# Sparse experts: two of three block tables made between the first eight blocks; a diagonal router and a scan in the prologue

## The reference, cut to what matters

```python
flat = x.reshape(-1, C)                       # 8192 x 64
logits = flat @ router_w.T                    # 8 experts
probs = jax.nn.softmax(logits, axis=-1)
topk_probs, topk_idx = jax.lax.top_k(probs, 2)
topk_probs = topk_probs / (jnp.sum(topk_probs, axis=-1, keepdims=True) + 1e-09)
gates = jnp.einsum('nk,nke->ne', topk_probs, jax.nn.one_hot(topk_idx, 8))
h = jax.nn.silu(jnp.einsum('nc,ehc->neh', flat, w1)) * jnp.einsum('nc,ehc->neh', flat, w3)   # 682 hidden
y = jnp.einsum('neh,ech->nec', h, w2)
out = jnp.einsum('ne,nec->nc', gates, y)
```

## Time and profile before

| what | value |
|---|---|
| median of 3 runs | 2289.25 us (2287.74 to 2291.01) |
| the profiled execution | 2279.4 us, of which the trace spans 2277.6 us |
| first stage (ffn2): first SyncE load / first row load of the second block | 1186.6 / 1271.2 us |
| second stage (ffn3): the same | 1790.2 / 1873.7 us |
| mean granted TensorE clock | 0.839 of full speed |

### The profile page before, as it was taken

The page is one execution under the profiler, slowest core; times in us unless marked ns, Lnnn a source line. Parts: engine busy times, 40 slices in busy tenths (PEclk is TensorE's granted clock), DMA queues, the critical chain, the costliest instruction groups (busy, mean ns, idle before and its releaser), DMA issues. The chain is left out here.

```text
span 2277.6 us, 30440 instructions
## 1 busy us (share of the span) xinstructions
PE 1677.3 (74%) x11157; PEld 967.5 (42%) x11157; DVE 1245.0 (55%) x2416; ACT 965.8 (42%) x1715; POOL 590.1 (26%) x591
## 2 busy tenths in 40 slices
PE   2899996897999970312304599999845539999994
PEld 2433333345333340100103366666545426666663
DVE  6643335655633357578787555555462565555554
ACT  2565653333655543325123244444322424444441
POOL 0100000001000000000005577743452157776332
PEclk8899997996999975556555799999967759999997
DMA  1322210002222200000000354444268014544444
GB/s 41 76 68 65 65 56 20 0 0 50 76 65 65 65 23 0 0 0 0 0 4 27 117 147 147 149 138 134 92 152 167 7 57 149 147 146 143 133 133 151
DMA packets 117333, 175.30 MB, mean 77 GB/s; under 512 B 38106, under 2 KB 66522, under 8 KB 116674
## 3 DMA queue, kind: packets, MB, share of 16 engines
q1 hardware_dynamic: 99906, 155.38, 23.8%
q0 software_dynamic: 17280, 17.99, 2.4%
HBM read 148.60 MB, written 24.70 MB: 76 GB/s over the span
## 5 line engine op out<-in xcount | busy, mean ns | idle before, releaser
L1350 DVE TENSOR_TENSOR ffn_hidden<-ffn_silu,ffn_up_ps 114x512 f32<-114x512 f32 x426 | 293.0, 688 | 349.9 <-ACT ffn_silu L1320 349.0
L1262 PE MATMUL ffn_up_ps<-ffn_turned,ffn_weights 64*114 64x256 f32 x3408 | 445.8, 394 | 5.8 <-DMA ffn_weights<-in_ffn_weights 4.9
L1320 ACT ACTIVATE ffn_silu<-ffn_up_ps 114x512 f32<-114x512 f32 x426 | 254.4, 597 | 388.9 <-PE ffn_up_ps L1262 386.5
L826 POOL DMA_INDIRECT slots<-ffn_rows,ffn_slot x256 | 251.7, 983 | 557.4 <-DVE ffn_slot L944 386.4
L736 ACT ACTIVATE ffn_hidden<-ffn_up_ps,ffn_b 128x512 f32<-128x512 f32 x512 | 310.1, 689 | 198.0 <-PE ffn_up_ps L631 198.0
L1241 POOL DMA_INDIRECT results<-ffn_yout,ffn_xin x284 | 271.9, 957 | 246.0 <-DVE ffn_yout L1338 179.6
L1262 PEld LDWEIGHTS ffn_up_ps<-ffn_turned,ffn_weights 64*114 64x114 f32 x3408 | 288.1, 176 | 110.6 <-issue 59.6
L631 PE MATMUL ffn_up_ps<-ffn_T,ffn_up_w 64*128 64x512 f32 x1024 | 261.2, 623 | 3.1 <-ACT ffn_hidden L736 3.1
L652 PE MATMUL ffn_y_ps<-ffn_hidden,ffn_down 128*64 128x512 f32 x1024 | 247.9, 605 | 3.4 <-DVE ffn_y_total L526 3.4
L1273 PE MATMUL ffn_y_ps<-ffn_hidden,ffn_weights 114*64 114x256 f32 x1704 | 215.2, 388 | 0.0
L526 DVE SCALAR_TENSOR_TENSOR ffn_gated<-ffn_y_ps,ffn_b,ffn_gates 128x512 f32<-128x512 f32 x96 | 72.0, 751 | 204.7 <-PE ffn_y_ps L652 203.1
(11 more groups left out here) (412 smaller groups left out, 2067.1 us busy)
## 6 DMA issues: line engine op xcount, KB each, us to landing
ffn_weights<-in_ffn_weights SPq DMA_DIRECT2D x142, 534.0 KB
ffn_gates<-gate_rows SPq DMA_DIRECT2D x128, 256.0 KB
ffn_xin<-slots SPq DMA_DIRECT2D x142, 66.0 KB
sht_mix<-in_sht_weights SPq DMA_DIRECT2D x8, 1024.0 KB, 8.4
results<-ffn_yout,ffn_xin POOLq DMA_INDIRECT x284
slots<-ffn_rows,ffn_slot POOLq DMA_INDIRECT x256
D<-results SPq DMA_DIRECT2D x16, 256.0 KB, 5.4
ffn_second<-results SPq DMA_DIRECT2D x16, 256.0 KB, 5.9
```

What stands on the lines that cost most here:

```text
L826: nc.gpsimd.indirect_dma_start(k.slots, bass.IndirectOffsetOnAxis(slot[c][:, t:t + 1], 0), rows[c][:, t, :], None).then_inc(row_stored[h], 16)
L1262: last = nc.tensor.matmul(up_ps[w][n % 2][0:SIZE, chunk % 2 * BLOCK:(chunk % 2 + 1) * BLOCK], weights[rows_of, b % WEIGHTS, chunk * SIZE:( ...
L1320: nc.scalar.activation(silu[0:SIZE, n % 2, :], up_ps[0][n % 2][0:SIZE, :], ACT.Silu).then_inc(silu_done, 1)
L1350: nc.vector.tensor_tensor(hidden[0:SIZE, b % 2, c, :], silu[0:SIZE, n % 2, :], up_ps[1][n % 2][0:SIZE, :], ALU.mult).then_inc(hidden_done, 1)
```

## The change

1. `table(i)` is split into four portions, `count_blocks` (4 instructions), `take_blocks` (6), `table_experts` (3) and `table_places` (5, one of which, the update of `passed`, is now made for the last phase too). For phase 0 all four still run in the prologue. For phases 1 and 2 VectorE runs one portion after each of the first eight blocks of the second program block.
2. SyncE reads the tables in spans that begin at the phases (`SPANS`, seven instead of six), and ahead of the spans at blocks 0, 9 and 25 it waits for `tabled`, which the last instruction of each table raises.
3. The router is laid out by the host as a 128 x 16 block-diagonal matrix. A pair of tiles takes one matmul of 128 rows and 16 columns; `choose` takes both halves with one copy.
4. The doubling steps are replaced by one scan over (expert, tile): `adds` is laid expert by expert, and `goes_on` is 1 everywhere but at the first tile of an expert, where it is 0 (four small memsets, which take the place of two).
5. What the portions need lives in `TableMemory`, in the outer scope, beyond the prologue.

```diff
-TURN = 13
+SPANS = ((0, 9), (9, 17), (17, 25), (25, 37), (37, 48), (48, 60), (60, ALL_SLOTS))
...
+        def table_places(ch, i):
+            nb = PHASES[i]
+            past, weighed = (x[:, 0:E * nb].rearrange("p (e b) -> p e b", e=E) for x in (t.wide, t.weighed))
+            ch.link(nc.vector.tensor_tensor(weighed, past, t.steps[:, :].unsqueeze(2).to_broadcast([P, E, nb]),
+                                            ALU.mult))
+            ch.link(nc.vector.tensor_reduce(t.place_f[:, 0:nb], weighed.rearrange("p e b -> p b e"), AX.X, ALU.add))
+            ch.link(nc.vector.scalar_tensor_tensor(t.place_f[:, 0:nb], t.place_f[:, 0:nb], t.passed[:, 0:1],
+                                                   numbers[:, 0:nb], ALU.add, ALU.add))
+            ch.link(nc.vector.tensor_tensor(t.passed[:, 0:E], t.passed[:, 0:E], t.taken[:, :], ALU.add))
+            nc.vector.tensor_copy(block_place[:, PHASE_AT[i]:PHASE_AT[i] + nb], t.place_f[:, 0:nb])\
+                .then_inc(tabled, 1)
...
                     dve.wait_ge(multiplied, t1 // (2 * GROUP))
-                    for half in (0, 1):
-                        product = small_ps[h][half][:, t0 // 2 * E:t1 // 2 * E].rearrange("p (t e) -> p t e", e=E)
-                        ch.link(nc.vector.tensor_copy(r.L[:, t0 + half:t1:2, :], product))
+                    ch.link(nc.vector.tensor_copy(r.L[:, t0:t1, :].rearrange("p t e -> p (t e)"),
+                                                  small_ps[h][:, t0 // 2:t1 // 2, :, :]
+                                                  .rearrange("p i h e -> p (i h e)")))
...
-                    ch.link(nc.vector.tensor_copy(r.run[0][:, 32, :], first))
-                    ch.link(nc.vector.tensor_copy(r.run[0][:, 33:32 + n, :], totals[:, 0:n - 1, :]))
-                    i, step = 0, 1
-                    while step < n:
-                        a, b = r.run[i], r.run[1 - i]
-                        ch.link(nc.vector.tensor_tensor(b[:, 32:32 + n, :], a[:, 32:32 + n, :],
-                                                        a[:, 32 - step:32 + n - step, :], ALU.add))
-                        i, step = 1 - i, 2 * step
-                    until = r.run[i]
-                    ch.link(nc.vector.tensor_tensor(pl, until[:, 32:32 + n, :], before, ALU.add))
+                    adds, until = (x[:, 0:E * n].rearrange("p (e t) -> p t e", e=E) for x in (r.adds, r.until))
+                    ch.link(nc.vector.tensor_copy(adds[:, 0, :], first))
+                    ch.link(nc.vector.tensor_copy(adds[:, 1:n, :], totals[:, 0:n - 1, :]))
+                    ch.link(nc.vector.tensor_tensor_scan(r.until[:, 0:E * n], r.goes_on[h][:, :], r.adds[:, 0:E * n],
+                                                         0.0, ALU.mult, ALU.add))
+                    ch.link(nc.vector.tensor_tensor(pl, until, before, ALU.add))
...
-                table(0)
+                count_blocks(ch, 0)
+                take_blocks(ch, 0)
+                table_experts(ch, 0)
+                table_places(ch, 0)
                 choose(1)
                 gates(1)
                 place(1)
-                table(1)
-                table(2)
+                k.chained = ch.n
...
-                        for half in (0, 1):
-                            rows_of = slice(half * CH, (half + 1) * CH)
-                            last = nc.tensor.matmul(small_ps[h][half][:, pair * E:(pair + 1) * E],
-                                                    ring[rows_of, g % 2, i * P:(i + 1) * P], router[rows_of, :],
-                                                    start=True, stop=True)
+                        last = nc.tensor.matmul(small_ps[h][:, pair, :, :].rearrange("p h e -> p (h e)"),
+                                                ring[:, g % 2, i * P:(i + 1) * P], router[:, :],
+                                                start=True, stop=True)
...
-                for first in range(0, SLOT_BLOCKS, TURN):
-                    count = min(TURN, SLOT_BLOCKS - first)
+                for first, end in SPANS:
+                    count = end - first
+                    if first in PHASE_AT:
+                        sp.wait_ge(tabled, PHASE_AT.index(first) + 1)
                     places, experts = registers(block_place, first, count), registers(block_expert, first, count)
...
+                    if b < 8:
+                        (count_blocks, take_blocks, table_experts, table_places)[b % 4](ch, 1 + b // 4)
```

More of the change, by code:

```diff
@@ L784 @@
 CONST_COLS = const_columns()
-class RouteMemory:
+class TableMemory:
     def __init__(self, sb):
         self.consts = sb("consts", [P, CONST_COLS])
[L790 to L794, removed]
         self.ends, self.blocks, self.taken, self.steps = (
@@ L804, in const, with __init__ @@
         return self.consts[:, CONSTS[n][0]:CONSTS[n][1]]
+class RouteMemory:
+    def __init__(self, sb):
+        self.L, self.marked, self.soft, self.G, self.F, self.S, self.place = (
+            sb(n, [P, TILES, E]) for n in ("L", "marked", "soft", "G", "F", "S", "place"))
+        self.top, self.mark, self.g1, self.g2, self.total, self.below_one = (
+            sb(n, [P, TILES]) for n in ("top", "mark", "g1", "g2", "total", "below_one"))
+        self.adds, self.until = (sb(n, [P, E * TILES]) for n in ("adds", "until"))
+        self.goes_on = [sb(f"goes_on{h}", [P, E * (t1 - t0)]) for h, (t0, t1) in enumerate(RANGES)]
 def sparse_stage(nc, sem, k, name):
@@ L823, in sparse_stage, with count_blocks @@
         spares_stored = sem(f"{name}_spares_stored")
-        def store_row(h, c, t):
-            nc.gpsimd.indirect_dma_start(k.slots, bass.IndirectOffsetOnAxis(slot[c][:, t:t + 1], 0),
-                                         rows[c][:, t, :], None).then_inc(row_stored[h], 16)
+        numbers = t.const("numbers")
+        def count_blocks(ch, i):
+            m = min(LANDED[i][1] * P // BLOCK, REGION - 1)
+            whole = i < len(PHASES) - 1
+            count = t.counts[:, i, :]
+            short = t.wide[:, 0:E * m].rearrange("p (e i) -> p e i", e=E)
+            ch.link(nc.vector.tensor_scalar(count, count, 1.0 / BLOCK, None, ALU.mult))
+            ch.link(nc.vector.tensor_tensor(short, numbers[:, whole:m + whole].unsqueeze(1).to_broadcast([P, E, m]),
+                                            count.unsqueeze(2).to_broadcast([P, E, m]),
+                                            ALU.is_le if whole else ALU.is_lt))
+            ch.link(nc.vector.tensor_reduce(t.blocks[:, :], short, AX.X, ALU.add))
+            ch.link(nc.vector.tensor_tensor(t.blocks[:, :], t.blocks[:, :], t.passed[:, 0:E], ALU.subtract))
@@ L829, in sparse_stage, with store_row @@
+        def store_row(h, c, tile):
+            nc.gpsimd.indirect_dma_start(k.slots, bass.IndirectOffsetOnAxis(slot[c][:, tile:tile + 1], 0),
+                                         rows[c][:, tile, :], None).then_inc(row_stored[h], 16)
         with ExitStack() as inner:
@@ L996, in _ @@
+                        ch.link(nc.vector.tensor_tensor(t.counts[:, 2, :], t.ends[:, :], region, ALU.subtract))
                 centre(0)
@@ L1234, in _ @@
                 for i in (1, 2):
[L1235 removed]
+                    for tile in range(*LANDED[i]):
                         for c in (0, 1):
[L1237 removed]
+                            store_row(i, c, tile)
                 for b in range(SLOT_BLOCKS):
```

112 lines of the change are left out of this document (45 added, 67 removed).

## The result

The changed kernel takes 2267.15 us (median of 4 runs, 2254.28 to 2269.15); the kernel before, run beside it, takes 2290.13 us (one of its four executions took 7328.6 us and stands in that median; the median of the other three is 2289.25). The ratio is 0.9896, with a 95% interval from 0.9874 to 0.9917: 1.0% faster. The forecast was 2269.7 us, 19.6 us less than before; measured it is 23.0 us less (22.1 by those three), and in a second comparison 2267.53 against 2289.44 us, 21.9 less, ratio 0.9908 [0.9892, 0.9925].

The account below looks back on a forecast made before the run. VectorE was taken to end last in the prologue, 6.25 us over SyncE. 6.25 + 4.65 - 1.1 = 9.8 us a stage, 19.6 in all, gave a median of 2269.7 us, range 2264 to 2278.5.

Parts of the forecast that it names:

- Tables out of the prologue: End of the prologue: 10.75 us of VectorE work leave, 6.25 us a stage show, since SyncE becomes the last.
- `ends` earlier: Prologue chain of VectorE and TensorE up to `ends`, which SyncE waits for: 4.65 us a stage shorter.
- (a): First range of the prologue: a scan over 128 elements replaces four doubling steps, gain 0.8 us.
- (d): `choose`: one copy instead of two gains 0.2 us in each range, four memsets for two lose 0.2; together 0.2 us.
- (b): Second range of the prologue: a scan replaces the doubling steps of 3.55 us, gain 2.55 us.
- (c): Router on TensorE ahead of `choose(1)`: one 128-row matmul a pair shortens the last stretch, gain 1.1 us.
- Portions: Table portions between the second program block's blocks exceed VectorE's cover and delay TensorE: 1.1 us a stage lost.
- A: Prologue and blocks: `ends` gains under 2 us a stage, or portions stick out by 3 or more; 2278.8 us, chance 0.12.
- B: Router: the product falls to half, up to VectorE's cap, 2.7 us more a stage; 2264.3 us, chance 0.08.
- C: Prologue's end: SyncE's table loads run into its padding stores, the block starts 2 us later; 2273.7 us, chance 0.10.
- D: First blocks: portions make TensorE pause and its clock stays at 1.2 GHz; slower, 2352 us, chance 0.03.
- E: Prologue's end: another wait, on GpSimd, say, holds the barrier where it was; within 0.2% only if nothing moved, chance 0.02.

Follow-up runs that it names:

- the two halves: Against the kernel before: only the late tables moved out of the prologue, 2271.71 us; only the new router and scan, tables back in the prologue, 2277.42 us.
- e1: The kernel before with only the two late tables moved between the blocks, old router and doubling steps kept: 2271.71 us, ratio 0.9927.
- e4: The kernel before with both router matmuls of a pair on the same 64 rows, leaving out the routing of every second tile: 2313.1 us.
- e7: The change with each late table made in one piece, behind blocks 2 and 5: 2292.99 us in a single run.
- e9: The change with padding stores behind the first loads and the first phase's last eight scatters at the second block's front: 2274.54 us, single run.

## Why the prediction was right, and where its sizes were off

Both main steps hold, and the two halves tried alone show them. The row load was forecast 10.9 us earlier and came 10.95; that it is so close is luck, since `ends` gave 0.4 us less than its sum and the way behind it some 0.5 more, a term that the sum did not have. For the profiled execution the forecast was 2259.8 us and it took 2266.17, for it lost 10.2 us ahead of the sparse stages. By the terms:

- **Tables out of the prologue, 6.25 us.** Right: SyncE became the last (its wait fell from 13.2 to 0.3 us), and e1 gave 6.90 and 7.25. Most of the surplus is the way from there to the row load, 2.16 us where it was 2.63, a term that I had at nothing; in the second stage SyncE also stood further ahead of VectorE than 6.25 us, 6.45 (74.41 against 80.86).
- **`ends` earlier, 4.65 us.** Measured 4.24 and 4.32. (a) and the first range's part of (d): from the router's copy to the last slot 10.57 us before and 9.68 after, less 0.28 us that the copy starts later behind the four memsets: 0.6 us, where 0.8 + 0.2 - 0.2 was forecast. (b) From the first copy of `place(1)` to the cast 7.96 us before, 5.88 after: 2.1, not 2.55. (c) and the copy of (d), 1.2 + 0.3 us, against 1.1 + 0.2. What failed is the size in (a) and (b): the scan at 0.80 us, and the strides at half of their upper bound. The scan takes 0.96 us for 384 elements and 0.42 for 128, and the rows decide against the reduce that I had taken for it. The Trainium skill, page "DVE: opcode table, instruction layouts, handler registers and perf-mode slots", section "Datapath and trigger behaviour", says that the built-in scan runs at half throughput; the estimate by it was 0.42 and 0.96 us, and the trace agrees. The strides cost their upper bound, 0.24 us each, since a strided pass of 384 takes 0.80.
- **Portions, 1.1 us lost.** Measured about 0.6 in each stage: 0.31 behind block 7, 0.33 and 0.19 behind block 0 (where 0.3 was forecast), and in the second stage 0.08 behind block 6. The term that was too large is block 7, at 0.7. I had let the cover end where the next product's idle ended. But VectorE takes the first instruction behind a portion about 0.1 us ahead of the portion's end in the records (1318.57 against 1318.66), and I had not worked out the cover of the fold, which is what was late behind block 7, not the product.
- **The rest.** TensorE's first two blocks took 10.49 us instead of 11.28 in the first stage, the wait behind block 0 included, and in the second the way from the first row load to the first `up` was 0.46 us shorter. Nothing in the change asks for that, and its cause is open. The first two blocks vary without the change too: 11.28 and 10.45 us in the two stages before, 10.40 and 11.54 in e4, which has the padding stores and the tables where they were. In the second stage the sum is complete: the first chunks of `up` begin 11.71 us earlier (88.62 to 76.91), the first two blocks take 10.76 instead of 10.45 us, 0.39 are lost behind blocks 6 and 7, and the 11.0 remain.

Of the rivals, **A** fell: 4.2 and not under 2 us from `ends`, 0.6 and not 3 in the blocks. **B** fell: a product of eight takes 1.73 us, as the hyperbolic row had it, and e4 shows why. The total came out near B's all the same, for other reasons, and a total by itself would not have told. **C** was the wrong way round: the way from the barrier's last engine to the row load got shorter, 2.16 us instead of 2.63. **D** did not happen at pauses of 0.2 to 0.33 us (the window from 1300 to 1650 us has the granted clock at 1.00), but e7 shows that it is real from 2.65 us. **E** fell, though it was close: GpSimd, which I had put at 1253.2 with 4 us to spare, arrives some 2.5 us later than its last scatter says. SyncE's end hid it by 0.3 us. That was luck, for I had read the end of an engine's last instruction as its arrival.

## What to carry to other kernels

Where engines meet at a barrier, list the end of each, move the last one's work under cover, and price only the distance to the second; then everything that this second one waits for counts at once. An engine's last instruction is not always its arrival: GpSimd came 2.5 us behind its own. Work moved between the blocks of a saturated loop must be cut to the idle time of its engine there: in portions of 1 to 2 us it cost 0.6 us a stage, in two pieces of 4.7 and 6.3 us it cost 12, nearly half of it through the clock. And count a matmul's records by what they overlap with, not by their number: 32 on alternating row halves cost what 16 on all rows do.

## What the runs showed of the hardware that I had not expected

- The scan, 0.42 us for 128 and 0.96 us for 384 elements, costs 1.4 and 1.7 times a plain pass of the same size (0.29, 0.56).
- A pass over fp32 that crosses its tensor with a stride takes 0.79 or 0.80 us for 376 and 384 elements instead of 0.55 or 0.56, whether the stride is on what it writes (the copy) or on what it reads (the sum).
- TensorE's granted clock was 0.56 over the 6 us behind a pause of 2.65 us (e7), after more than 10 us of work at full clock, and was back at 1.00 in the next window.
- GpSimd reached the barrier some 2.5 us later than its last scatter instruction let one think (3.60 us to the next block when it was last, 1.1 us for VectorE in e9), and one of its 32 scatters took 2.53 or 0.96 us from one execution to the next, which moved its end by 1.2 us.
- A router record of 64 rows costs what one of 128 rows does, 0.218 and 0.214 us, unless it alternates with the other 64 rows, 0.112.
- The same unchanged stages took 10.2 us more in one execution than in another, all ahead of the first sparse stage, so that a difference of two profiled spans shows 13.2 us of a gain of 23.
